# Fused four-head attention: the order of TensorE's work within a step, and where its waits stand

## The reference

```python
q = _split_heads(jnp.einsum('bfe,ed->bfd', x, W_query))
k = _split_heads(jnp.einsum('bfe,ed->bfd', x, W_key))
v = _split_heads(jnp.einsum('bfe,ed->bfd', x, W_value))
attn = jax.nn.softmax(jnp.einsum('hbqd,hbkd->hbqk', q, k), axis=-1)
out = jnp.einsum('hbqk,hbkd->hbqd', attn, v)     # heads joined again
y = jax.nn.relu(out + jnp.einsum('bfe,ed->bfd', x, W_res))
```

## Time and profile before

| | |
|---|---|
| median of three runs | 1635.06 us |
| the profiled execution | 1633.92 us, span 1632.1 us |
| busy share of the span | TensorE 98%, VectorE 74%, ScalarE 67%, GpSimd 57% |
| mean granted TensorE clock | 0.994 of full speed |
| chain that ended last | TensorE 98% |

### The profile page before, as it was taken

One profiled execution on the slowest core, in us unless ns is written; L12 is line 12 of the kernel. 1 busy time (PEld: TensorE's weight loads), 2 busy tenths in 40 slices (PEclk: granted clock), 3 DMA queues, 4 the chain that ended last, 5 costly groups with the idle time before them and its releaser, 6 DMA issues.

```text
span 1632.1 us, 95535 instructions
## 1 busy us (share of the span) xinstructions
PE 1606.5 (98%) x41984; PEld 1541.2 (94%) x41984; DVE 1200.2 (74%) x1537; ACT 1096.1 (67%) x1794; POOL 932.6 (57%) x1290
## 2 busy tenths in 40 slices
PE   6999999999999999999999999999999999999997
PEld 6999999999999999999999999999999999999996
DVE  4677777777777777777777777777777777777774
ACT  3676666667676766666676767666676767666664
POOL 2555555565655555565656555555656555555655
PEclk9999999999999999999999999999999999999998
DMA  2222222222223222222222232222222222322221
GB/s 59 76 83 89 83 85 84 84 84 84 84 84 88 83 87 84 84 84 84 84 84 86 83 89 83 86 84 84 84 84 84 84 88 82 88 84 84 84 84 54
DMA packets 271797, 135.33 MB, mean 83 GB/s; under 512 B 9312, under 2 KB 271712, under 8 KB 271712
## 3 DMA queue, kind: packets, MB, share of 16 engines
q1 hardware_dynamic: 270336, 134.25, 28.0%
q10 hardware_dynamic: 1376, 0.26, 0.1%
HBM read 67.37 MB, written 67.11 MB: 82 GB/s over the span
## 4 chain that ended last, share of the span: by engine, by line
PE 98%; issue 1%; DVE 0%; ACTq 0%; DMA 0%; ACT 0%; POOLq 0%; POOL 0%; DVEq 0%
PE ps_so L242 17%; PE ps_pt L231 16%; PE ps_so L220 13%; PE ps_qk L196 8%; PE ps_qk L198 8%; PE ps_qk L197 8%; PE ps_vr L209 8%; PE ps_vr L210 7%; PE ps_vr L211 7%; PE ps_x L186 7%; DMA w_raw<-in_L_rec_W_res_dram 0%; ACTq L334 0%; POOLq L39 0%; DVE attn L378 0%; DVE x_lo L351 0%
## 5 line engine op out<-in xcount | busy, mean ns | idle before, releaser
L150 POOL TENSOR_TENSOR y<-attn,vr 128x256 f32<-128x256 f32 x512 | 341.4, 688 | 596.3 <-issue 585.2
L308 ACT COPY probs_t<-ps_pt 128x512 f32<-128x512 f32 x512 | 302.0, 590 | 423.3 <-PE ps_pt L231 423.2
L362 DVE TENSOR_REDUCE row_max<-ps_so 128x16 f32<-128x1024 f32 x256 | 313.5, 1225 | 339.7 <-PE ps_so L242 339.5
L156 POOL TENSOR_SCALAR y<-y 128x512 f32<-128x512 f32 x256 | 380.7, 1487 | 22.4
L292 ACT COPY qk<-ps_qk 128x512 f32<-128x512 f32 x512 | 301.1, 588 | 65.0 <-PE ps_qk L198 13.9
L196 PE MATMUL ps_qk<-x_hi,w_hi 128*128 128x256 f32 x1024 | 332.7, 325 | 5.6 <-DVE x_lo L351 3.3
L231 PE MATMUL ps_pt<-ident,probs 128*128 128x128 f32 x2048 | 323.2, 280 | 0.8 <-ACT probs_t L308 0.7
L300 ACT COPY vr<-ps_vr 128x512 f32<-128x512 f32 x512 | 297.8, 582 | 33.8 <-PE ps_vr L211 1.5
L367 DVE TENSOR_TENSOR shifted<-ps_so,row_max 128x1024 f32<-128x1024 f32 x256 | 313.5, 1225 | 8.8
L209 PE MATMUL ps_vr<-w_hi,x_hi 128*128 128x256 f32 x1024 | 310.8, 304 | 0.1
L242 PE MATMUL ps_so<-vr,probs_t 64*64 64x33 f32 x8192 | 293.0, 222 | 4.2 <-issue 2.8
(11 more groups left out here) (23 smaller groups left out, 2249.0 us busy)
## 6 DMA issues: line engine op xcount, KB each, us to landing
x_in<-in_r_x_dram SPq DMA_DIRECT2D x256, 256.0 KB, 2.8
out_dram<-y SPq DMA_DIRECT2D x256, 256.0 KB, 2.3
w_raw<-in_L_rec_W_query_dram ACTq DMA_DIRECT2D x1, 64.0 KB, 3.1
w_raw<-in_L_rec_W_key_dram ACTq DMA_DIRECT2D x1, 64.0 KB, 3.7
w_raw<-in_L_rec_W_value_dram ACTq DMA_DIRECT2D x2, 32.0 KB, 3.2
w_raw<-in_L_rec_W_res_dram ACTq DMA_DIRECT2D x2, 32.0 KB, 2.5
```

The lines of the kernel that those rows point to most:

```text
L150: nc.gpsimd.tensor_tensor(y[:, n % 2, a * HALF:(a + 1) * HALF].rearrange("k t (p j d) -> k j (t p) d", j=2, d=D), attn[:, n % 2, a * HALF: ...
L156: nc.gpsimd.tensor_scalar(y[:, n % 2], y[:, n % 2], 0.0, None, ALU.max).then_inc(y_ready, 1)
L362: nc.vector.reduce_max(row_max[:, :].rearrange("q (h u) -> q h u", h=HEADS), scores, AX_X).then_inc(max_ready, 1)
```

## The change

On TensorE the step's pieces come in another order. The weighted values go ahead of the scores; the transposes of x stand behind the first transposes of probabilities, ahead of the q/k projection. The second half of the value/residual projection is cut in two: its first three matmuls, then the four waits (each for one body later than at the head of the old step, so for the same values as before), then its other three. On VectorE the wait for `o_done` (weighted values finished) goes from the row maximum to the reciprocals.

```diff
-            def project_vr(i, n, a):
-                if a == 1 or has(i - 1):
+            def project_vr(i, n, a, tiles=range(HALF)):
+                if tiles[0] == 0 and (a == 1 or has(i - 1)):
                     pe.wait_ge(vr_ready, halves(i, a) - 1)
...
-                for t in range(HALF):
+                for t in tiles:
...
-                last.then_inc(vr_done, 1)
+                if t == HALF - 1:
+                    last.then_inc(vr_done, 1)
...
             def step(i, n):
-                if has(i - 1):
-                    pe.wait_ge(shifted_ready, i)
-                if has(i - 3):
-                    pe.wait_ge(attn_ready, i - 2)
-                if has(i - 2):
-                    pe.wait_ge(pt_ready, halves(i - 2, 1))
-                    pe.wait_ge(v_moved, (i - 2) * 2 + 2)
-                if has(i):
-                    pe.wait_ge(qk_ready, halves(i, 1))
-                    score(i)
                 if has(i - 2):
                     weigh_values(i - 2, (n + 2) % RING, 0)
                     weigh_values(i - 2, (n + 2) % RING, 1).then_inc(o_done, 1)
+                if has(i):
+                    pe.wait_ge(qk_ready, halves(i, 1))
+                    score(i)
                 if has(i - 1):
                     pe.wait_ge(probs_ready, i)
                     transpose_probs(i - 1, 0)
+                if has(i + 2):
+                    transpose_x(i + 2, n)
...
                 if has(i + 1):
                     project_qk(i + 1, (n + 1) % RING, 1)
-                if has(i + 2):
-                    transpose_x(i + 2, n)
-                if has(i):
-                    project_vr(i, n, 1)
+                if has(i):
+                    project_vr(i, n, 1, range(0, 1))
+
+                if has(i):
+                    pe.wait_ge(shifted_ready, i + 1)
+                if has(i - 2):
+                    pe.wait_ge(attn_ready, i - 1)
+                if has(i - 1):
+                    pe.wait_ge(pt_ready, halves(i - 1, 1))
+                    pe.wait_ge(v_moved, (i - 1) * 2 + 2)
+                if has(i):
+                    project_vr(i, n, 1, range(1, HALF))
...
                     dve.wait_ge(s_done, i + 1)
-                    if has(i - 2):
-                        dve.wait_ge(o_done, i - 1)
                     nc.vector.reduce_max(...)
...
                 if has(i - 2):
-                    if not has(i):
-                        dve.wait_ge(o_done, i - 1)
+                    dve.wait_ge(o_done, i - 1)
                     nc.vector.reciprocal(...)
```

More of the change, by code:

```diff
@@ L248, in step @@
             def step(i, n):
-                if has(i - 1):
-                    pe.wait_ge(shifted_ready, i)
-                if has(i - 3):
-                    pe.wait_ge(attn_ready, i - 2)
                 if has(i - 2):
-                    pe.wait_ge(pt_ready, halves(i - 2, 1))
-                    pe.wait_ge(v_moved, (i - 2) * 2 + 2)
+                    weigh_values(i - 2, (n + 2) % RING, 0)
+                    weigh_values(i - 2, (n + 2) % RING, 1).then_inc(o_done, 1)
                 if has(i):
@@ L258, in step @@
                     score(i)
-                if has(i - 2):
-                    weigh_values(i - 2, (n + 2) % RING, 0)
-                    weigh_values(i - 2, (n + 2) % RING, 1).then_inc(o_done, 1)
                 if has(i - 1):
```

## The result

The changed kernel takes 1644.74 us, the median of four runs (1644.1 to 1646.21), against 1634.74 for the kernel before beside it: ratio 1.0064, 95% interval 1.0046 to 1.0081. It is slower by 10 us. Forecast were 1645.5 us and a slowdown of 10.6. The sum came out right by luck: the mechanism was right, but two terms were off by about the same amount in opposite directions.

What follows compares the result with a forecast made beforehand. TensorE was taken as the bound, busy for 1528.00 of 1528.00 us. The only term counted, a late weight load of 256 x 3/4 x 0.055 = +10.6 us, raised 1635.06 to 1645.7, stated as 1645.5; range 1629 to 1661.

Steps and rivals of the forecast that it cites:

- Part 1: TensorE, x transposes beside transposes of probabilities: gain 0, at most 0.08 us a step by recorded durations.
- Part 2: TensorE, values ahead of scores: again three tile-shape changes, no change, -0.05 to +0.05 us a step for two unseen junctions.
- Part 3: Pieces from the first q/k half on come 0.44 us later; second probabilities copy ends at 806.18 instead of 805.74.
- Part 4: Weight load behind the four waits comes 0.05 to 0.06 us late in three of four steps: +10.6 us.
- so each adds about 0.06: Each wait instruction between a late event and the weight load adds about 0.06 us, from 0.05 without and 0.11 with one.
- Part 5: VectorE without its second wait: `attn` ends at about 806.03, ahead of the probabilities copy at 806.18; worth nothing.
- No wait ends late anywhere in the steady part.: Kernel before: TensorE busy 1528.00 of 1528.00 us, so waits are hidden and only fewer or shorter TensorE pieces could gain.
- The sum: Steady loss 10.6 us, ends 0 with 3 us either way: 1635.06 + 10.6 = 1645.7, stated as 1645.5 us.
- A: Rival, no stall: waits fall in another order or the copy comes 0.05 us earlier; 1635 us, chance 0.29.
- B: Rival, faster: one 0.36 us matmul behind transposes goes away, 20.5 us, 1614.6; or cheaper values-to-scores, 1622; chance 0.15.
- C: Rival, larger stall: two sequencer instructions behind the late one every step, or copy held longer; 31 us, 1666, chance 0.10.

Runs made afterwards that it cites:

- xoldpt: Changed kernel with the `pt_ready` wait written first and the x transposes back behind the second q/k half; 1626.4 us, ratio 0.9957 to the kernel before.
- ptcar: Changed kernel with only the order of its four waits altered, `pt_ready` written first; 1624.17 us, ratio 0.9936 to the kernel before.
- xonly: Kernel before with only the x transposes moved behind the first transposes of probabilities; 1637.89 us, ratio 1.0032.
- dose: Changed kernel with two more waits, on events long past, beside the four; 1641.38 us, ratio 1.0051 to the kernel before.
- bmid: Kernel before with only its four waits moved into the middle of the second value/residual half; 1638.56 us, ratio 1.003.
- w4: Changed kernel with its four waits one matmul later, ahead of the fifth of six value/residual matmuls; 1629.55 us, ratio 0.9966 to the kernel before.

## Why the prediction was right, and where it was not

- **Part 1, adjacency worth 0: right.** xoldpt against ptcar tests it with no stall in the way, and xonly from the other side. In the change the eighth transpose starts at 806.30 + 0.60 - 0.27 = 806.63 and the second projection matmul at 806.86, 0.23 later, as forecast. The 0.36 us of a first matmul behind transposes was an artefact of the record.
- **Part 2, three tile-shape changes worth 0: right.** xoldpt has values first and takes 6.227 us a step. The junctions after: projection to values is 0.20 (797.43 to 797.63), values to scores 0.15 (last weighted value at 804.82, scores at 804.97), scores to transposes 0.15 (last score at 805.66, transposes at 805.81), against 0.21, 0.15 and 0.15 in the earlier trace rows.
- **Part 3, what x pushes back: right.** The second copy of probabilities ends 796.86 - 791.11 = 5.75 us after the last projection matmul of the step before; forecast 5.75. xonly shows the q/k stall that values-first hides.
- **Part 4, the stall behind the waits: mechanism right, size too small.** The form of the waits in three of four steps is the one forecast. The step that failed is "so each adds about 0.06". From the earlier trace rows I had one place with a wait instruction (0.11 us from event to load) and one without (0.05), and took every further one to cost the same. The first does cost 0.06; the others cost nearly twice as much:

  | sequencer instructions from the late event to the load | us | where |
  |---|---|---|
  | 0 | 0.05 |; xonly |
  | 1 | 0.11 | |
  | 2 | 0.23 | the change, three steps (797.09 - 796.86) |
  | 3 | 0.33 | the change, fourth step (803.35 - 803.02) |
  | 4 | 0.42 | dose, fourth step |

  The late wait itself is counted. The one exception is the other three steps of dose, 0.17 with two, where the late wait had already begun. In the change the load comes 0.23 behind the copy instead of 0.17, and the loss is 0.09, not 0.055.
- **Part 5, VectorE out of the race: right in three steps, wrong in the fourth.** `attn` ended where forecast (796.70 - 791.11 = 5.59, forecast 5.60). But I ranked the engines by when their events come. What counts is the event plus all that stands between it and the load: 5.60 + 0.33 is later than 5.75 + 0.05. The fourth step was forecast to lose nothing and loses 0.04. For the same reason the change on VectorE is not "worth nothing": in bmid, without it, `attn` ends 0.1 us later and the fourth step loses 0.12 on average. bmid has the old order too, and the VectorE edit was not run alone.
- **"No wait ends late anywhere in the steady part."** I took this from a busy time of 1528.00 of 1528.00 us. For the kernel before (6.230 us a step) it holds as far as the runs show, since none of them has a step below 6.227, but the reason does not: the change, with 0.09 us lost in three of four steps, shows 1539.00 of 1539.00.
- **The sum.** Forecast 192 x 0.055 = 10.6 us steady and 0 at the ends. Measured 256 x 0.075 = 19 steady and about 9 back at the ends, which I had bounded by 3 us either way. The total agrees only because the two errors cancel, which is luck.
- **The rivals.** A (no stall) and B (adjacency gains) are excluded by the steps. C expected 0.12 us in every step, from two sequencer instructions behind the late one; the loss is 0.09 with one behind it in three steps, and 0.04 in the fourth.

## What to carry to other kernels

Where several waits stand in front of one instruction and little is queued ahead of them, see in the trace which wait the instruction itself carries, and make it the late one; here a reordering of source lines, with no other edit, turned a ratio of 1.0064 into 0.9936. When an engine is never idle in the profile, its busy share cannot show such a loss; compare distances between starts instead: 0.09 us in each of three steps hid inside a busy share of 100%. Waits hide only behind what is queued in front of them, so place them where the matmuls queued ahead outlast the last event plus every wait instruction after it.

## What the runs showed of the hardware that was not expected

A satisfied wait instruction behind a late one costs 0.09 to 0.11 us of the way to the next weight load, although it is recorded with 51 ns. In front of the late one it costs nothing: in ptcar two of them stand there and the step is 6.233.

The loop's turn is not free where little is queued. In w4 the step at whose end the loop goes back to its start takes 6.27 us in place of 6.23, and its last gap, from the last projection matmul to the first weighted value, is 0.25 in place of 0.21:

```profile
814.98 0.28 PE L211 MATMUL ps_vr<-w_hi,x_lo 128*128 128x256 f32 x1
815.23 0.21 PE L243 MATMUL ps_so<-vr,probs_t 64*64 64x33 f32 x1
```

```profile
L103 PEldq COMPARE_BRANCH  x1: 215/215/215, 814.9 to 814.9; - x1
```

The branch is recorded with 215 ns and stands behind the waits in TensorE's program; here it ends at 815.09, and the first load of the values comes at 815.20. With two matmuls between the waits and the step's end this shows, 0.04 us every four steps; with three, as in ptcar, it does not. That the branch is the cause was not tested by a run of its own.
